# First group of each attention: row maxima made for query tiles 0 to 3 and 4 to 7 apart, with the units of the first half of the queries beside the remaining chunks

## What is computed

```
# layer 1, H = 16, dh = 8, n = 1024
q = _rotate(q, cos, sin); k = _rotate(k, cos, sin)
s = jnp.einsum('bhqd,bhkd->bhqk', q, k) / math.sqrt(dh)
s = jnp.where(causal, s, -jnp.inf)
a = jax.nn.softmax(s, axis=-1)
o = jnp.einsum('bhqk,bhkd->bqhd', a, v).reshape(b, n, d)
...
# layer 2: the same sizes, no mask
attn = jax.nn.softmax(scores, axis=-1)
ao = jnp.einsum('bhqk,bhkd->bhqd', attn, v)
```

## Time and profile before

| | us |
|---|---|
| three timed executions | 1825.01, 1814.08, 1824.59 |
| their median | 1824.59 |
| the profiled execution's own time | 1819.02 |
| its span, first to last instruction | 1817.2 |
| granted TensorE clock, mean of the span | 0.907 |
| PE, DVE, ACT, POOL busy | 1483.6, 1278.4, 1165.3, 376.9 |

### The profile page before, as it was taken

One profiled execution on the slowest core, in us unless ns is written; L12 is line 12 of the kernel. 1 busy time (PEld: TensorE's weight loads), 2 busy tenths in 40 slices (PEclk: granted clock), 3 DMA queues, 4 the chain that ended last, 5 costly groups with the idle time before them and its releaser, 6 DMA issues.

```text
span 1817.2 us, 39113 instructions
## 1 busy us (share of the span) xinstructions
PE 1483.6 (82%) x15249; PEld 676.9 (37%) x15249; DVE 1278.4 (70%) x1974; ACT 1165.3 (64%) x2370; POOL 376.9 (21%) x415
## 2 busy tenths in 40 slices
PE   4669999999999788569999998999887898649970
PEld 2324444444443455212222222222221236538870
DVE  7787777777773465799999998999776752322244
ACT  4627777777677555239998987898765684213331
POOL 3400000000000455200000001001223211664273
PEclk9859899999899999769999999999987898869985
DMA  3513422121111344300100120111001304435763
GB/s 118 181 69 111 142 82 92 39 86 62 58 41 43 114 122 128 134 6 31 37 31 32 49 73 25 36 47 53 31 32 41 112 13 134 134 106 186 228 199 107
DMA packets 132776, 152.94 MB, mean 84 GB/s; under 512 B 13744, under 2 KB 107824, under 8 KB 132336
## 3 DMA queue, kind: packets, MB, share of 16 engines
q1 hardware_dynamic: 122480, 123.43, 21.8%
q0 software_dynamic: 10112, 27.01, 4.0%
HBM read 90.90 MB, written 63.46 MB: 85 GB/s over the span
## 4 chain that ended last, share of the span: by engine, by line
PE 46%; DVE 23%; issue 9%; ACT 9%; DMA 5%; SPq 4%; another core or an unknown queue 2%; POOL 1%; ACTq 0%; POOLq 0%; DVEq 0%
DVE row_max L624 17%; PE bank L593 16%; PE banks L569 10%; PE banks L537 6%; PE banks L1408 4%; ACT probs L678 4%; PE banks L1398 4%; DMA qk_parts<-parts 2%; SPq L487 2%; DMA q_work<-max_T 2%; PE banks L577 1%; ACT max_T L669 1%; ACT o_sums L689 1%; PE banks L324 1%
## 5 line engine op out<-in xcount | busy, mean ns | idle before, releaser
L624 DVE TENSOR_REDUCE row_max<-banks 128x2 f32<-128x1024 f32 (+3 forms) x896 | 940.5, 1104 | 168.4 <-PE banks L543 74.1
L678 ACT ACTIVATE probs<-banks 128x512 f32<-128x512 f32 (+3 forms) x1792 | 880.3, 551 | 214.2 <-PE banks L569 100.4
L593 PE MATMUL bank<-probs,v_ones 128*32 128x256 f32 (+3 forms) x7168 | 543.0, 381 | 20.0 <-ACT o_sums L689 16.6
L569 PE MATMUL banks<-q_work,k_work 51*128 51x512 bf16 (+3 forms) x1792 | 392.0, 376 | 62.9 <-ACT probs L678 28.5
L537 PE MATMUL banks<-k_work,q_work 48*128 48x512 bf16 (+3 forms) x1792 | 371.0, 384 | 74.2 <-DVE row_max L624 59.3
L569 PEld LDWEIGHTS banks<-q_work,k_work 51*128 51x128 bf16 x1792 | 103.2, 93 | 440.5 <-ACT probs L678 338.0
L716 POOL DMA_DIRECT2D heads_out<-o_sums x64 | 35.7, 557 | 1094.3 <-ACT o_sums L689 1094.3
L593 PEld LDWEIGHTS bank<-probs,v_ones 128*32 128x32 f32 x7168 | 147.9, 110 | 263.3 <-ACT probs L678 184.8
L1994 ACT ACTIVATE rope<-banks,expert 128x256 f32<-128x256 f32 x184 | 72.2, 475 | 185.1 <-PE banks L1398 92.1
L537 PEld LDWEIGHTS banks<-k_work,q_work 48*128 48x128 bf16 x1792 | 95.2, 96 | 139.3 <-DVE row_max L624 108.4
L1408 PE MATMUL banks<-expert,rope 128*128 128x128 f32 x736 | 100.4, 295 | 26.4 <-DVE k_work L1711 14.9
(11 more groups left out here) (206 smaller groups left out, 1161.3 us busy)
## 6 DMA issues: line engine op xcount, KB each, us to landing
expert<-expert_rows SPq DMA_DIRECT2D x46, 578.0 KB
qk_parts<-parts SPq DMA_DIRECT2D x64, 256.0 KB, 3.3
heads_out<-o_sums POOLq DMA_DIRECT2D x64, 256.0 KB, 4.2
q_work<-qk_parts SPq DMA_DIRECT2D x64, 128.0 KB
k_work<-qk_parts SPq DMA_DIRECT2D x64, 128.0 KB
sorted_in<-zeros SPq DMA_DIRECT2D x4, 1472.0 KB, 12.1
parts<-sorted_in SPq DMA_DIRECT2D x22, 256.0 KB
probs<-in_x SPq DMA_DIRECT2D x16, 256.0 KB, 3.6
```

The source lines that it names most:

```text
L569: last = pe.matmul(to[par][:, 0:G - c0], k[r:r + M1, pair, kt * P:(kt + 1) * P], q[r:r + M1, pair, qh * G + c0:(qh + 1) * G], start=True, ...
L593: last = pe.matmul(bank[7][32 * j:32 * j + 32, c0 + part * w:c0 + (part + 1) * w], v_ones[i % QB][:, kt, j, :], prob_slots[:, (e + j) % RI ...
L624: dve.tensor_reduce(row_max[:, qt, 2 * pair:2 * pair + 2, kh], self.buf_of("chunk", g, c)[:, :, 0:width], AX.X, ALU.max).then_inc(s["chunk ...
L678: act.activation(prob_slots[:, e % RING, 0:width], banks46[:, e % EXP_BANKS, 0:width], ACT.Exp, scale=SCALE).then_inc(s["exps"], 1)
```

## The change

The plan becomes a list of events for each group, with the group of each event in it, in place of one list with offsets. Three things come out of this.

1. For group 0 the maxima are made in two parts. Part 0 (query tiles 0 to 3) follows the first half of the chunks: 8 of 24 in the causal attention, 16 of 32 in the other. Then come two chunks, the transposes of part 0, four chunks, and unit 0. Beside the units of queries 0 to 511 stand the last 10 chunks of group 0, the maxima of part 1, chunks (1,0) and (1,1), and the transposes of part 1. The first unit of queries 512 to 1023 waits for the DMAs of part 1.
2. Beside the second half of group 0's units stand the chunks of group 1 from the third on, its maxima, and six chunks of group 2 with the transposes between: 30 events on 16 units in the causal attention, 38 on 16 in the other.
3. Events of groups past the last are left out before the spreading, not skipped in it. Beside the units of group 14 stand 20 events on 24 units (before: places for 26), and 28 on 32 (before: 34), and the transposes of group 15 are the last of them.

The groups 1 to 13 keep their order. The core of the diff:

```diff
-    stream = [("chunk", 1, c) for c in range(LEAD, n)] + [("maxima", 1, 0)]
-    stream += [("chunk", 2, c) for c in range(LEAD)]
-    stream.insert(n - LEAD + 1 + COVER, ("transposes", 1, 0))
...
+    half = sum(chunk[0] < GT for chunk in chunks)
+    units = [PAIRS * k + pair for k in range(len(steps)) for pair in range(PAIRS)]
+    early = sum(PAIRS for step in steps if step[0] == 0)
+
+    def row(g, part, upto):
+        return ([("chunk", g, c) for c in range(COVER)] + [("transposes", g - 1, part)]
+                + [("chunk", g, c) for c in range(COVER, upto)])
+
+    def along(i, some_units, stream):
+
+        out, c = [], 0
+        for k, u in enumerate(some_units):
+            out.append(("unit", i, u))
+            upto = (k + 1) * len(stream) // len(some_units)
+            out += stream[c:upto]
+            c = upto
+            if u >= PAIRS:
+                out.append(("values", i, u - PAIRS))
+        return out
+
+    last = [("values", u) for u in units[-PAIRS:]]
+    events = {-1: [("chunk", 0, c) for c in range(half)] + [("maxima", 0, 0)]
+              + [("chunk", 0, c) for c in range(half, half + COVER)] + [("transposes", 0, 0)]
+              + [("chunk", 0, c) for c in range(half + COVER, half + LEAD)]}
+    for i in range(NG):
+        rest = [("chunk", i + 1, c) for c in range(COVER if i == 0 else LEAD, n)] + [("maxima", i + 1, 2)] + row(i + 2, 2, LEAD)
+        rest = [event for event in rest if event[1] < NG]
+        if i == 0:
+            first = [("chunk", 0, c) for c in range(half + LEAD, n)] + [("maxima", 0, 1)]
+            first += [("chunk", 1, c) for c in range(COVER)] + [("transposes", 0, 1)]
+            events[i] = along(i, units[:early], first) + along(i, units[early:], rest)
+        else:
+            events[i] = along(i, units, rest)
+        events[i] += [(what, i, u) for what, u in last]
...
+            def tiles(self, part):
+
+                return slice(0, NQT) if part == 2 else slice(part * GT, (part + 1) * GT)
...
             def sp(self, sp, between=None, before=None):
-                self.sp_maxima(sp, 0)
+                for part in range(HALVES):
+                    self.sp_maxima(sp, 0, part)
...
-                    if u == 0:
-                        pe.wait_ge(s["max_in"], 64 * (i + 1))
+                    if u == 0 and i:
+                        pe.wait_ge(s["max_in"], 64 * (self.turned(i, 2) + 1))
+                    if i == 0 and kt == 0 and pair == 0:
+                        pe.wait_ge(s["max_in"], 64 * (self.turned(0, qh) + 1))
```

More of the change, by code:

```diff
@@ L130, in build @@
+    return chunks, steps, events, half
 def build(nc, t, out):
@@ L597, in values @@
                     last.then_inc(s["values"], 1)
[L599 to L600 removed]
                 for i in range(-1, NG):
[L602 to L603 removed]
+                    for what, g, n in self.events[i]:
+                        if what == "unit":
                             unit(i, n)
@@ L691, in act @@
                 for i in range(-1, NG):
-                    for what, ahead, n in self.order:
-                        if what == "unit" and i >= 0:
+                    for what, g, n in self.events[i]:
+                        if what == "unit":
                             unit(i, n)
```

137 lines of the change are left out of this document (63 added, 74 removed).

## The result

| | before | after |
|---|---|---|
| median | 1823.01 | 1855.57 |
| lowest and highest of four | 1814.08, 1825.01 | 1852.36, 1868.85 |
| profiled execution, its span | 1819.02, 1817.2 | 1856.79, 1855.0 |
| granted clock, mean of the span | 0.907 | 0.892 |

The changed kernel is slower by 2.12% (ratio 1.0212, 95% interval 1.0174 to 1.0251). The forecast was 1841, slower by 0.9 to 1.0% (21 us by its sum, set on the mean of four executions, and so 18 above the median). The time lies inside the range, 1825 to 1857, but at its upper end.

What follows compares the result with a forecast made beforehand. DVE alone was taken to bound each attention's start, with PE, DVE and ACT nearly full after it. Terms 8 + 4 + 5 + 4 = 21 us on the four executions' mean of 1820.7 gave 1841, range 1825 to 1857.

Steps and rivals of the forecast that it cites:

- DVE bounds the second attention's start, and the head start is worth nothing: Second attention: unit 0 starts 19.2 us earlier, but DVE's fixed reduces make group 1's unit 0 about 8 us later.
- The rival that keeps the head start: Both attentions' starts: unit 0's 19.2 and 14.2 us are kept, -14 us in all, 1805; chance 0.06.
- Second attention, +8: Second attention's start: unit 0 of group 1 at about 849.8 against 841.7; bounds +5 and +11.
- the upper bound: Second attention's start: +11 us, if PE at half clock in the second half makes DVE wait too.
- The low bound of +5: Second attention's start: +5 us, if units 0 to 15 go faster with fewer chunks and the copy is short.
- The rival by which most of the shift is taken up: Second attention's start and both ends at their low costs: 13 us in all, 1832 to 1834; chance 0.24.
- First attention, +4: First attention's start: unit 0 of group 1 at 156.3 against 152.56; bounds +1 and +8.
- DMAs start at 103.7 and unit 0 at 107.7: First attention: part 0's DMAs start behind the projection's last stores, unit 0 14.2 us earlier than 121.88.
- My upper bound of 8: First attention's start: +8 us, with the short chunks' gaps as in their rows and a slower DMA behind the stores.
- End of each attention, +5 and +4: Last group: later last chunk and transposes delay group 15's unit 0; bounds +2.9 to +7 (first), +2 to +6 (second).
- The waits drop the clock: Rival: four new waits of 3 to 5 us lower PE's clock, about three times 2.5 us more, 1848; chance 0.2.
- The high bounds: All four terms at their upper bounds: 11 + 8 + 7 + 6 = 32 us on 1824.6, giving the range's end 1857.

Runs made afterwards that it cites:

- e7: Changed kernel with the last groups' order restored and part 1's maxima and transposes moved up beside the first half's last four or six units; ratio 1.0072 to the kernel before.
- e8: e7 and e3 together: waits covered, loads and stores behind the DMAs, last groups' order restored; ratio 1.005 to the kernel before.
- e3: Changed kernel with the projection's last load and two last stores issued on SP behind part 0's four DMAs; ratio 1.0202 to the kernel before.
- e10: Kernel before with only the third part of the change, group 14's events spread over all its units; ratio 1.0059, or 10.7 us.
- e1: Changed kernel with its third part undone, so group 14 has its order of before; ratio 1.0191 to the kernel before.
- e6: Changed kernel with 16 unused pairs of chunk matmuls on PE ahead of group 0's second half and of group 15; ratio 1.018 to the kernel before.
- half reduces: Each row maximum reads only the first half of its chunk's columns; ratio 0.9786 on the kernel before, 0.9983 on the changed kernel, both to the kernel before.
- e12: Kernel before with COVER = 1 in place of 2, the transposes one chunk earlier; ratio 0.9826, 1787.1 us.
- e13: e8 with COVER = 1; ratio 0.9843 to the kernel before.
- e14: Changed kernel with COVER = 1; ratio 1.0035 to the kernel before.
- e15: Kernel before with COVER = 0, the transposes directly behind the maxima; ratio 0.9851.

## Where the prediction was right, and which of its steps failed

1. *DVE bounds the second attention's start, and the head start is worth nothing.* Right: unit 0 came 19 us earlier and unit 0 of group 1 later. e7 and e8 show it from the other side. The rival that keeps the head start fell.
2. *Second attention, +8; measured +11.0.* The steps to unit 16 hold within 0.6 us. The step that failed is "DVE bounds" for the 31 reduces and a maxima behind unit 16 at 36.3 us without gaps. They took 39.8: DVE waits six times for a PE at a clock of 0.60, and this stretches 43.5 to 46.7. I had named it as the upper bound and left it out of the sum. Covering the wait in e7 takes 9.6 off. The low bound of +5 was mis-worked: 17 x 1.107 = 18.8 leaves nothing to gain on the 18.9 that I took for units 0 to 15, and with fewer chunks beside them they took 18.7 (806.46 to 825.16). The rival by which most of the shift is taken up rested on this too, and fell.
3. *First attention, +4; measured +13.3.* The step that failed, and the largest error of the whole prediction, is "DMAs start at 103.7 and unit 0 at 107.7". The start of the DMAs was right, the landing wasn't: it took 8.57, where I had the 1.8 of a queue with nothing ahead. I had seen the stores and priced their issue on SP (1.49 us), and not the transfer of what SP had issued before, the loads and stores that were still under way. e3 gives 7.6 for it, e7 3.9 for the wait ahead of unit 8, and 1.9 stay in e8. My upper bound of 8 allowed for a slower DMA, with far too little.
4. *End of each attention, +5 and +4.* Right within its bounds, +6.0 and +3.1: alone about 10.7 us by e10. Of the 6.0, 3.3 are the later place of the copy at full clock and 2.7 a fall of the clock. e1, without the new order, has as long a fall there, so these 2.7 aren't priced by the working, and that the term came out near 5 is in part luck.
5. *The waits drop the clock.* In the second start this is open. The clock behind the wait was 0.60, and it wasn't hidden by DVE, as the prediction had it, but cost about 3 us. Filling the wait didn't lift it (e6, 0.63), and an order without the wait did (e7, 0.91). In the first attention's last group filling the wait gives 1.0 us, but the clock was no better there before, behind a wait of 1.78 (0.88, against 0.86 after). The trace of before has a second case of a long wait that I missed, 5.37 us at 1372.15: three units at half clock, then full clock again. By the Trainium skill ("TensorE: Matmul & The Clock Gate", the section on the HAM clock gate) sustained activity is what lifts the clock. No run here shows whether that is what e7 has and e6 lacks.
6. *The sum.* 13.3 + 6.0 + 11.0 + 1.9 + 1.2 = 33.4 for 21. 9.3 of the 12.4 missing are the first attention's start, most of it one DMA's landing; 3 the second's. The high bounds had added up to 32, less than the five stretches. That the time still lies in the range, 1.4 us below its end, is luck: one term went 5 beyond its bound, the second start lies at its bound, and the ends stayed below theirs.

What stays open: why the price of the first start doesn't fall with half reduces, what holds the clock at 0.60 in the second half of group 0, and what makes groups 1 to 14 of the second attention up to 12 us longer in some profiles.

## What to carry to other kernels

Overlap that starts a stage earlier gains only if the engine that bounds the stage gets through its work earlier; count that engine's instructions to the next common point, and price every new wait by what it makes that engine idle. A small DMA on a path that sets the end must be priced with all bytes queued ahead of it, not with its issues. Where a wait recurs at the same place in every group, moving its producer by one slot is a cheaper first try than a new split: here it was worth 1.7%, and the split cost 2.1%.

## What the runs showed of the hardware beyond that

A wait of 1.3 to 1.8 us ahead of each group of the first attention is followed by a stretch at half clock in about half of the groups, in all kernels here with `COVER` = 2: group 14 of the first attention began behind 1.45 us in the kernel before and ran at 1.00, and behind 1.46 in the changed one and ran at 0.90. In the kernel before, `max_T` copies of the first attention:

```profile
147.61 1.01 ACT L669 ACTIVATE max_T<-banks 12x1024 bf16<-12x1024 bf16 x1
...
176.09 1.01 ACT L669 ACTIVATE max_T<-banks 12x1024 bf16<-12x1024 bf16 x1
...
207.47 1.01 ACT L669 ACTIVATE max_T<-banks 12x1024 bf16<-12x1024 bf16 x1
...
238.69 1.01 ACT L669 ACTIVATE max_T<-banks 12x1024 bf16<-12x1024 bf16 x1
```

The periods are 28.5, 31.4 and 31.2; over the attention short and long ones mix. In e12 they are all 27.7 to 27.8:

```profile
146.79 1.00 ACT L669 ACTIVATE max_T<-banks 12x1024 bf16<-12x1024 bf16 x1
...
174.44 1.00 ACT L669 ACTIVATE max_T<-banks 12x1024 bf16<-12x1024 bf16 x1
...
202.25 1.00 ACT L669 ACTIVATE max_T<-banks 12x1024 bf16<-12x1024 bf16 x1
```

PE's waits for these DMAs, before and in e12 (total us, times, longest), and the windows of the whole attention, before and in e12:

```profile
PE banks L569 <- DMA q_work<-max_T: 22.2, 15, 1.8
```
```profile
PE banks L569 <- DMA q_work<-max_T: 7.8, 15, 1.0
```
```profile
91.00:598.00 507.00, 453.32 (x6774) 203.78 (x6775) 370.85 (x473) 361.97 (x817) 25.68 (x49) 0.91 0.23 74
```
```profile
91.00:568.00 477.00, 436.20 (x6773) 198.39 (x6774) 369.79 (x473) 361.33 (x817) 25.47 (x48) 0.95 0.25 79
```

The waits shrink by 14.4 us in all and PE's busy time by 17.1, from the clock, for the same instructions; the attention is 28 us shorter between its copies 1 and 14. The two kinds of period differ by 2.7 us, so a wait of 1.5 can cost 2.7 more than itself. The other runs bear this out: from copy 1 to 14 the first attention takes 360.9 to 361.8 in all four kernels with `COVER` at 1 or 0 (e12, e13, e14, e15), and 386.9 to 395.2 in all kernels with 2 and full reduces. That it is the shorter wait, and not the earlier place of the transposes in some other way, is argued and not shown; filling these waits was not tried.

Also not expected: the copy of 12 x 512 elements took 0.59 us against 1.01 for 12 x 1024; and a 3 KB DMA that lands in 1.7 to 1.8 us took 8.57 behind the loads and stores of one projection.
